# ScalarE's queue takes over the sample-column transfers, attention blocks alternate between two PSUM banks, and a block's four window numbers come in one register load

## The reference

```
x  = x + dwconv3(x)
q, kv = layernorm(x) @ qkv_w                 # 49 windows of 8x8 pixels per image
idx = top4(mean(q) . mean(k))                # each window picks 4 windows of keys and values
o   = softmax(q . k[idx]) @ v[idx]           # 4 heads, 64 queries x 256 keys a window
x  = x + (o + dwconv5(v)) @ wo ;  x = x + mlp(layernorm(x))
# second layer, with feat_s a small map resized to 56x56
feat = relu(conv1x1(x * (1 + gate)))
off  = relu(conv1x1([feat, feat_up * 2]))
dy, dx, mask = conv3(off)                    # 72 sample points (8 groups x 9 taps) a pixel
out = relu(deformable_conv3(feat_up, dy, dx, mask)) + x
```

## Time and profile before

| | us |
|---|---|
| median of 3 runs | 13883.27 (13882.18 to 13892.24) |
| profiled execution: time | 13886.23 |
| profiled execution: span from first to last instruction | 13883.2 |
| PE busy | 10537.0 (76%) |
| PE weight loads busy | 8028.7 (58%) |
| ACT busy | 8917.4 (64%) |
| DVE busy | 8448.6 (61%) |
| POOL busy | 6916.6 (50%) |
| granted TensorE clock, mean over the span | 0.918 |

### The profile page before, as it was taken

How to read it: one execution, slowest core, us unless ns; L and a number is a source line. 1 busy time by engine, 2 the same in 40 slices (tenths; PEclk the granted TensorE clock), 3 DMA queues, 4 the chain that set the end, 5 groups by cost and what they waited for, 6 DMA issues and landing times.

```text
span 13883.2 us, 501225 instructions
## 1 busy us (share of the span) xinstructions
PE 10537.0 (76%) x187900; PEld 8028.7 (58%) x187900; DVE 8448.6 (61%) x11589; ACT 8917.4 (64%) x18708; POOL 6916.6 (50%) x6167
## 2 busy tenths in 40 slices
PE   3567887878787787878778787877878787741787
PEld 2346665666666666666666666666666666631666
DVE  6446667575666657576666757666675766631743
ACT  1246666667666676766666676666667666741677
POOL 0024554545455454545445454544545454566467
PEclk7679999999999999999999999999999999976999
DMA  4134444445444444444444444444444444431444
GB/s 127 47 78 112 117 113 114 114 109 122 109 117 113 115 116 109 122 110 118 113 116 115 109 121 110 118 111 118 115 109 119 112 118 111 120 75 29 107 128 115
DMA packets 1847066, 1517.08 MB, mean 109 GB/s; under 512 B 1006688, under 2 KB 1381984, under 8 KB 1841568
## 3 DMA queue, kind: packets, MB, share of 16 engines
q1 hardware_dynamic: 1834468, 1474.31, 42.7%
q0 software_dynamic: 9216, 2.38, 0.2%
HBM read 1297.68 MB, written 178.25 MB: 106 GB/s over the span
## 4 chain that ended last, share of the span: by engine, by line
PE 29%; issue 18%; DVEq 12%; ACT 9%; DVE 9%; POOLq 8%; SPq 6%; POOL 6%; DMA 2%; ACTq 1%
PE bank_small L952 6%; DVEq L1478 6%; PE bank_scores L871 5%; PE bank_small L1003 5%; POOLq L658 4%; PE windows L982 4%; DVEq L1463 4%; DVE ol L1479 3%; POOLq L660 3%; POOL gbuf L729 2%; ACT hats L1193 2%; SPq L496 2%; PE bank_post L925 2%; ACT hats L1197 1%; SPq L493 1%
## 5 line engine op out<-in xcount | busy, mean ns | idle before, releaser
L1533 DVE TENSOR_TENSOR prod<-windows,wy 128x640 f32<-128x640 f32 x4032 | 3283.7, 818 | 2036.0 <-PE windows L982 1933.9
L982 PEld LDWEIGHTS windows<-fx,hats 64*64 64x64 f32 x129024 | 2661.1, 139 | 1363.0 <-issue 1292.5
L982 PE MATMUL windows<-fx,hats 64*64 64x80 f32 x129024 | 3293.8, 243 | 181.9 <-issue 148.2
L657 POOL TENSOR_TENSOR prod<-prod 128x768 f32<-128x768 f32 x1344 | 2487.0, 1850 | 1364.8 <-DVE prod L1533 1357.3
L1193 ACT ACTIVATE hats<-hats,cst 128x512 f32<-128x512 f32 x4032 | 2879.1, 714 | 166.6 <-DMA hats<-sample_columns 96.8
L1479 DVE SCALAR_TENSOR_TENSOR ol<-xpad,lepw,ol 128x448 f32<-128x448 f32 x2688 | 2442.1, 909 | 240.9 <-issue 8.0
L1197 ACT ACTIVATE hats<-hats 128x512 f32<-128x512 f32 x4032 | 2517.2, 624 | 6.8
L871 PE MATMUL bank_scores<-ksel,qbd 128*128 128x256 f32 x3136 | 963.7, 434 | 1035.4 <-DVE ob L1464 893.2
L659 POOL TENSOR_TENSOR prod<-prod 128x384 f32<-128x384 f32 x1344 | 1563.0, 1163 | 214.9 <-issue 26.8
L662 POOL TENSOR_TENSOR val<-prod 128x384 f32<-128x384 f32 x1344 | 1497.7, 1114 | 241.1 <-issue 156.2
L952 PE MATMUL bank_small<-wom,ofp 128*128 128x216 f32 x8064 | 1609.4, 355 | 0.0
(11 more groups left out here) (193 smaller groups left out, 13333.4 us busy)
## 6 DMA issues: line engine op xcount, KB each, us to landing
hats<-sample_columns SPq DMA_DIRECT2D x2688, 336.0 KB
ksel<-k_windows SPq DMA_DIRECT2D x3136, 32.0 KB
vsel<-v_windows SPq DMA_DIRECT2D x3136, 32.0 KB
fx<-map_columns SPq DMA_DIRECT2D x64, 420.0 KB
xpad<-in_x SPq DMA_DIRECT2D x17, 1568.0 KB, 13.3
q_windows<-qb SPq DMA_DIRECT2D x112, 224.0 KB, 2.6
k_windows<-kb SPq DMA_DIRECT2D x112, 224.0 KB, 3.5
v_windows<-vb SPq DMA_DIRECT2D x112, 224.0 KB, 3.2
```

The source lines that it names most:

```text
L657: pool.tensor_tensor(v[:, :, 0:n], v[:, :, 0:n], v[:, :, n:2 * n], ALU.add)
L982: last[h] = pe.matmul(o[m], hat[:, m], fx[XP * h:XP * h + XP, g, row:row + WR, :].rearrange("p r c -> p (r c)"), start=True, stop=True)
L1533: dve.tensor_tensor(o, x, w.unsqueeze(3).to_broadcast([128, 2, CP * WR, CG]), ALU.mult).then_inc(s_wm, 1)
```

## The change

Three things change, and several smaller ones make room for them.

1. `store_columns` and `spread_columns` move from SP's list to ACT's, word for word: the store at the end of slot q = 5, the spread at the end of the second slot of each group instead of the first.
2. Attention windows alternate between `bank_scores` and a new `bank_scores2` (`bank_of(w)`). The steps are set further apart: scores in slot 3w, maxes and exps 3w+1, turn 3w+2, copy 3w+3, pv 3w+4, scale 3w+5. `scores(w)` waits for `scale_heads(w-2)`. `exps` now waits for the earlier `turn`, `copy_turned` for the earlier `pv`, since `pr` and `pt` stay single. In DVE's slot, scale and maxes come ahead of the taps.
3. `keys_values` loads the four numbers of a window with one multi-register load and without the bounds check.

To free the bank, `bank_turned` goes: sample columns are turned into free columns of `bank_small`; the nine transposes of `val` go in five steps (two, two, two, two, one) into unused columns of the `hb` banks, at q = 5, 6, 7, 8 and at q = 0 of the tile after; DVE copies them to `valt` (now two buffers) right behind `weigh`, which first waits for them; PE's `windows` of two slots later waits for the copy. `deform` and `relu` of a tile come at q = 5, one tile later, and so `finish` and the tile's store.

The core of the diff (the loop in `body` is ACT's, at the end of a slot; `copy_samples` is DVE's):

```diff
-OM, PXT, VT, WD, WYH = 0, 2, (4, 5, 7), 8, 2
+OM, PXT, WD, WYH = 0, 2, 5, 2
+VT, NP = Q + 5, 5
-P0 = A0 + BSL + 1
+P0 = A0 + BSL + 3
...
-        bs, bv_, bm, bp = [ctx.enter_context(nc.psum_tensor(n, [128, 512], F32))
-                           for n in ("bank_scores", "bank_turned", "bank_small", "bank_post")]
+        bs, bs2, bm, bp = [ctx.enter_context(nc.psum_tensor(n, [128, 512], F32))
+                           for n in ("bank_scores", "bank_scores2", "bank_small", "bank_post")]
...
+        def bank_of(w):
+            return (bs, bs2)[w % 2]
...
-                for m in range(TOPK):
-                    v = sp.value_load(sel[0:1, w * TOPK + m:w * TOPK + m + 1], min_val=0, max_val=P2 - 1)
+                _, chosen = nc.values_load_multi_w_load_instructions(
+                    sel[0:1, w * TOPK:(w + 1) * TOPK], engines=[mybir.EngineType.SP], min_val=0, max_val=P2 - 1,
+                    skip_runtime_bounds_check_because="they are places of maxima among P2 logits")
+                for m, v in enumerate(chosen):
                     sp.dma_start(ksel[s][:, m * W2:(m + 1) * W2],
...
@@ def scores(i, w):
-                wait(pe, s_os, cnt(i, P2, w))
+                else:
+                    wait(pe, s_os, cnt(i, P2, w - 1))
...
+            def turn_samples(i, t, p, bank):
+                pe.wait_ge(s_vok, cnt(i, NT, t + 1))
+                for k in range(2 * p, min(2 * p + 2, KK)):
+                    mm = pe.transpose(bank[:, k % 2, SPARE:SPARE + 128], val[t % 2][:, k * 128:(k + 1) * 128], ident)
+                mm.then_inc(s_vt, 1)
...
@@ def windows(i, t, q):
+                if bi is not None:
+                    pe.wait_ge(s_ve, cnt(bi, NP * NT, NP * bt + p + 1))
...
@@ def x_first(i, n):
-                if 0 <= m < SWIN * P2 and m % SWIN == 0:
-                    scores(i, m // SWIN)
-                if 0 <= m < SWIN * P2 and m % SWIN == 2:
-                    pv(i, m // SWIN)
+                w = step_of(n, 4)
+                if w is not None:
+                    pv(i, w)
+                w = step_of(n, 0)
+                if w is not None:
+                    scores(i, w)
...
@@ def body(xi, di):
+                        if fi is not None and q == PXS:
+                            store_columns(fi, ft)
+                        si, sg = group_of(di, xi, t * NG + q // CPG + HR - 1)
+                        if si is not None and q % CPG == 1:
+                            spread_columns(si, sg // NG, sg % NG)
...
+            def copy_samples(i, t, p, bank):
+                dve.wait_ge(s_vt, cnt(i, NP * NT, NP * t + p + 1))
+                wait(dve, s_do, cnt(i, NT, t - 1))
+                k = min(2, KK - 2 * p)
+                dve.tensor_copy(valt[t % 2][:, 2 * p:2 * p + k, :], bank[:, 0:k, SPARE:SPARE + 128]).then_inc(s_ve, 1)
```

191 lines of the change are left out of this document (99 added, 92 removed).

## The result

The changed kernel takes 13817.4 us (median of 6, 13805.2 to 13847.8), the kernel before 13891.0 (median of 6): a ratio of 0.995, 95% interval 0.9937 to 0.9963. It is 0.5% faster, where 13,070 was forecast, in a range of 12,600 to 13,500. TensorE is busy for 10780.3 us instead of 10537.0, with the same 187900 instructions. So its idle time fell by 303 us, from 13883.2 - 10537.0 = 3346 to 13823.8 - 10780.3 = 3043, and its busy time took 243 of them back.

A forecast was written before the change was run, and what follows sets the result against it. The prediction took the serial chain through the one score bank as the limit, SP's queue right behind. Savings of 654 (attention), 130 (body 0) and 36 (last body) less 8 (tail) made 812 us: 13,070 us, range 12,600 to 13,500.

The forecast's parts named there:

- Two banks: Attention: PE's wait for ob goes; tile 25.2 + 2.0 + 1.0 + 0.7 = 28.9 us instead of 31.65, saving 654 us.
- the rest: Attention: the remainder of PE's tile beyond its work and the ob, pr and pt waits, falling from 0.95 to 0.7 us.
- Body 0: Body without deformable work: SP limits at 7.9 us a window, falls to 6.0, window 2.65 us shorter, saving 130 us.
- SP's relief in the bodies: Attention: SP falls from 30.6 to 22.0 us a tile and no longer limits; 30.6 was the floor otherwise.
- the rival of a dear issue: ACT's seven transfers a tile at 1.6 us each make the kernel slower: 14,500 us; chance 0.09.
- The last body: Last body: PE's 43.5 us wait for ACT's sample copies goes, 8 us taken back, 36 us saved.
- Other stages: Stages outside attention, 278 us an image: no change, 5 us an image either way, as PE covers ACT's added work.
- The second: Rival: DVE takes the chain over in attention, PE's new waits eat 2 of 2.9 us; 13,500 us; chance 0.15.
- The fifth: Rival: nothing happens, windows queue at the single pr and pt; 13,883 us within 0.2%; chance 0.03.
- The third: Rival: SP's time was nobody's wait; body 0 gives nothing, banks give 654 us; 13,200 us; chance 0.05.
- The fourth: Rival: waits for exponentials and copies go as well, attention tile 26.4 us; 12,440 us; chance 0.08.
- the sixth: Rival: slower, because issuing transfers on ACT is dear, 1.6 us each; 14,500 us; chance 0.09.

The follow-up runs named there:

- the best order: The changed kernel with maxima ahead of weigh, exponentials behind ACT's other slot work, and scale_heads ahead of weigh too: 13313.4 us, 0.9579.
- the swap alone: The kernel before with scale_heads moved ahead of the taps in DVE's slot, SP's list unchanged: 13747.3 us, 0.9891.
- the best version: The changed kernel with maxima and scale_heads ahead of weigh, exponentials behind ACT's other slot work, columns' transfers back on SP: 13201.7 us, 0.9498.

## Why the prediction was wrong

**The step that failed** is "Two banks", the sum of 28.9 us a tile, in two of its terms: "PE's own work stays at 25.2", and the rest of 0.7. Measured are 439.2 / 125 x 9 = 31.6. Term by term, the stretch of 440 us being 13.9 tiles: PE's own work was forecast at 25.2 and measured 359.53 / 13.9 = 25.9; `ob` 0 and 0.35; `pr` 2.0 and 1.8; `pt` 1.0 and 1.25; the rest 0.7 and, by what is left of 31.65, 2.35. The exponentials, of which the prediction was most wary, came out right. Within the rest, (18.4 + 8.8) / 13.9 = 1.96 us are the wait for the hidden units.

The start of the sum was off as well. It was read in the one image with the lowest clock in attention (0.953, beside a mean of 0.970), which hides half of what went wrong. By the means of the last table a tile fell apart into 24.5 us of PE's work and 6.6 of its idle time before, 31.1 in all, and into 25.8 and 5.8 after. So the idle time fell by 0.8 us a tile where the forecast took 6.45 - 3.7 = 2.75 off, and the lower clock added 1.3 where the forecast had nothing.

**The idle time: its cause** is a wait that the prediction saw only as PE's. It wrote that the maxima "come behind that slot's `weigh` and behind the taps of the slot before", and priced this at 0.7 us in PE's wait for the exponentials. It did not ask who else stands in ACT's list behind them. ACT stood 79.4 us an image at the exponentials, and the hidden units behind them came late. On the mean of the bodies PE's wait for `ob` fell from 49.7 to 5.0 us an image, and that for `hid` rose from 4.3 to 26.8, that for `pr` from 17.2 to 26.3. It is shown by moving the maxima (-350 us in all; idle time 81.0 to 69.3, and in the stretches shown `hid` 27.2 to 18.9 and `pr` 25.4 to 12.9) and by putting the exponentials behind the hidden units (-101 us, or -93 by the two ratios; idle time 69.3 to 65.4, `hid` to 9.7). One bank is no proof of it: there ACT's wait falls from 79.4 to 25.1 and PE's idle time stays (82.3).

**PE's work "stays at 25.2"** was wrong by the clock. The transposes are as many as before, but in slots 81 to 206 as many instructions took 358.2 us at a clock of 0.920 instead of 339.8 at 0.970, and one bank brings both back (341.5 at 0.970). These 18.4 us an image are more than the 11.3 that the idle time gave. The two-bank kernels with all their taps were granted 0.920 to 0.953 there, the three one-bank kernels of the table 0.970 to 0.973 (a fourth, the kernel before with the scaling first, 0.953). PE's idle time alone does not order the clocks: without the taps PE is idle for 44.0 us and has 0.977, and after, it is idle for 81.0 and has 0.920. What lets the clock fall stays open. That it takes back what a shorter wait gives is measured: the second bank with the best order leaves PE idle for 56.5 us, one bank with the scaling first for 68.8, and both stages take 407 us.

**Body 0** was near in size, 111 us for 130, and wrong in its cause. SP was said to be its limit. The load alone left 8.64 us a window, the scaling ahead of the taps brought 7.87 with SP untouched, and two banks 6.38 with one load. It was the chain; and at 7.87 it was still the chain, for the load and the swap together give 7.80, though SP's 7.9 us of issue a window made it look like SP.

**SP's relief in the bodies** was counted at nothing for itself and at a cap of 30.6 us a tile with the chain eased. That there is such a cap was right: the swap alone stays at 427.9 / 125 x 9 = 30.8 us a tile, with the load it goes to 29.7 (before: 31.1). That the load alone gives 0.9%, at the start of attention, was not foreseen; the stretch read was the middle of the stage, 3566 to 4000 us, and the 9.2 us for the values stand ahead of it. The Trainium skill, page "DMA: Bandwidth & Descriptors", section "Issuing engines are not separate DMA queues", says that to issue from several engines saves only the sequencer's time to start the transfers, usually small beside the transfers themselves. The prediction held SP's 30.6 us a tile against that, but those are the queue's whole time, register loads included, and not the time of a start. For the move of the columns' transfers the runs agree once SP has the one load: the move changed nothing with the order eased (13382.8 and 13388.3), and in the best version it cost 112 us. With SP's queue full it gave 82 us (13889.5 to 13807.8). The larger relief of that queue were the loads: with the order eased, three of them a window with their register instructions were 365 us (13747.3 to 13382.8).

**Transfers on ACT.** Two rows, the spread and the store of the kernel after:

```profile
L1233 ACTq DMA_DIRECT2D hats<-sample_columns x2688: 312/402/2106, 801.2 to 13786.5; - x192
```

```profile
L1224 ACTq DMA_DIRECT2D sample_columns<-pxs x448: 307/308/1143, 797.1 to 13765.9; - x150
```

0.40 and 0.31 us (medians) for 0.39 and 0.53 taken; the rival of a dear issue, at 1.4 us and more, is out. That ACT's issue costs the kernel something all the same, 112 us in the best version, is shown; how it does so is open. The copy on DVE, 0.387 us on the mean of four and one, was right too (2.0 us a tile taken, 1.94 measured). That DVE's load would grow by more, through the taps 22.7 us an image in attention, was missed: it came to 350.70 / 13.9 = 25.2 us a tile for 24.4.

**The last body** was forecast 36 us shorter and is 21 us longer. The wait for ACT's copies is gone. But `weigh` now waits for the transposes, these for POOL's check (33.5 us), and the windows for the copy and the hats, so that PE's idle time is as long as before (91 us for 88), and the lower clock added 17 us to its work. The transposes a slot later gave 15 us back, the flag work and the deformable product later 13. No kernel was run without the wait of `weigh` alone. The columns on ACT cost 6 us (10 with the load); the rest isn't taken apart.

**Other stages** were given zero with 5 us an image either way; slots 0 to 59 lost 7 and 206 to 252 won 2.5. In slots 9 to 52 all kernels with the new sample path have some 130 us and all with the old one 122 to 126, whatever stands around them, so the path is the cause. Of the 7.1 us between before and after, 4.2 are PE's busy time (114.3 for 110.1, clock 0.959 for 0.984). Which piece of the path it is stays open; it is neither the flags' place (132.5 us) nor the copies on DVE (130.0 us with them on ACT).

**The rivals.** The second, that DVE takes the chain over, had the mechanism and the place, at a chance of 0.15, and its price for the waits was right: it kept 0.9 us a tile of the idle time, and 0.8 were measured. It too left the clock out, and took the last body for 36 us shorter. The fifth, that nothing happens, came nearest in time, by luck: much changed and cancelled out, and by body 0 and the start of attention the kernel is still outside its 0.2%. The third had body 0's share wrong, though it was right that SP was nobody's wait there. The fourth and the sixth are out.

## What to carry to other kernels

Before adding a buffer to shorten a chain of steps over several engines, look at what stands ahead of each short step in its engine's list, and put it ahead of the long work that nobody waits for; here this gave 3.65% with one bank and SP's one load (0.9% by itself), and the second bank gave nothing in the long stage, neither without this order nor with it. Look at the granted clock by stage, too, before and after: TensorE's busy time for the same instructions is no constant, and here it took back 243 of the 303 us that TensorE's waits had lost. Read it as a mean over several repetitions of a stage, not in one. A wait has to be followed on the engine that waits as well: what is queued behind it, and who waits for that, because the same delay then turns up under other names. And where two limits stand close, as the chain and SP's queue, neither edit shows its worth alone (1.1% and 0.9% apart, 3.65% together). Last, an experiment that leaves work out can change the data, and with them the path that the program takes: look in its trace for what else is missing.

## What the runs showed of the hardware

- A tap on DVE takes 683/684/687 ns (least, median, most of 150) in body 0, where GpSimd is idle, and 683/685/2308 ns in attention, as in the timeline above, where a tap of 2.31 us and a GpSimd instruction start together at 3724.64. The Trainium skill, page "SBUF — State Buffer", section "Who interferes with whom", has a DVE instruction with two SBUF inputs contend with a GpSimd one that reads SBUF; the trace agrees (a mean of 1.04 us in attention, where GpSimd is busy 212 of 440 us). Over the whole execution 1468 taps have no GpSimd instruction beside them and take 685 ns on the mean, 690 at most; the 1220 that overlap one take 1423 ns on the mean.
- A transfer issued from ACT's list takes about as long to issue as from SP's: 0.40 us for a spread and 0.31 for a store, beside 0.39 and 0.53 on SP.
- The same 187900 TensorE instructions were busy for 10537.0 us at a mean clock of 0.918 and for 10780.3 at 0.901. In slots 81 to 206 the busy time goes with the clock: 339.8 us at 0.970 and 358.2 at 0.920, a ratio of 1.054 in both.
- Four register loads from SP in one multi-register load take 293/300/732 ns (least, median, most of 784, after), where each single one takes 225/268/700.
